# First layer's scatters limited to four under way, and two expert set-ups with other buffers and loads

## The reference

```python
xn = layernorm(x)
x = x + L0_attn(xn) + L0_ffn(xn)      # gated linear attention (8 heads, chunks of 64) with its own
                                      # gated hidden layer; 14 experts of 176 hidden, best 2 of each token,
                                      # and a shared expert of 352 hidden
xn = layernorm(x)
x = x + L1_attn(xn) + L1_ffn(xn)      # state space model, 48 heads of 64, state 128;
                                      # 16 experts of 96 hidden, best 2 of each token
```

## Time and profile before

| | us |
|---|---|
| three runs | 3090.74, 3104.93, 3109.07 |
| median | 3104.93 |
| the profiled execution, its own time | 3097.32 |
| its span, first to last instruction | 3095.5 |
| mean granted TensorE clock | 0.938 of full |

### The profile page before, as it was taken

One profiled execution on the slowest core, in us unless ns is written; L12 is line 12 of the kernel. 1 busy time (PEld: TensorE's weight loads), 2 busy tenths in 40 slices (PEclk: granted clock), 3 DMA queues, 4 the chain that ended last, 5 costly groups with the idle time before them and its releaser, 6 DMA issues.

```text
span 3095.5 us, 58605 instructions
## 1 busy us (share of the span) xinstructions
PE 2693.5 (87%) x17318; PEld 2112.8 (68%) x17318; DVE 2383.3 (77%) x5972; ACT 2125.2 (69%) x4682; POOL 1976.0 (64%) x1697
## 2 busy tenths in 40 slices
PE   3698889886739978378799999999999999999997
PEld 2366666664539855267578788787787878878786
DVE  2466666664457769657699999999899999999996
ACT  3454454541245556445489999999899999999996
POOL 2232212225304413555489999999999999999998
PEclk8799898997869999689899999999999999999999
DMA  5455455464566545445777786666766666666663
GB/s 135 110 180 171 152 185 172 149 203 151 179 178 200 170 169 157 163 135 175 222 255 234 225 254 207 214 206 208 228 205 214 207 213 220 204 216 204 200 216 115
DMA packets 320411, 588.35 MB, mean 190 GB/s; under 512 B 47863, under 2 KB 138775, under 8 KB 319607
## 3 DMA queue, kind: packets, MB, share of 16 engines
q1 hardware_dynamic: 305750, 545.07, 56.5%
q0 software_dynamic: 14352, 39.54, 3.4%
HBM read 464.44 MB, written 124.17 MB: 190 GB/s over the span
## 4 chain that ended last, share of the span: by engine, by line
POOL 35%; issue 10%; ACT 3%; DVE 2%; POOLq 1%; PE 1%; DMA 0%; SPq 0%; ACTq 0%; DVEq 0%
POOL mm L2684 8%; POOL y L2697 7%; POOL yz L2701 7%; POOL y_lo L2690 6%; POOL y L2711 6%; ACT mt L2614 1%; DVE cv L2767 1%; POOLq L2360 1%; ACT ys L2628 0%; ACT mt L2634 0%; DVE bank L2838 0%; ACT L2649 0%; POOL first L2726 0%; DMA wi<-ssm_wi_split 0%; DVE xd L2829 0%
## 5 line engine op out<-in xcount | busy, mean ns | idle before, releaser
L2684 POOL TENSOR_TENSOR mm<-mt,cb 128x512 f32<-128x512 f32 x384 | 492.5, 1305 | 56.0 <-ACT mt L2634 53.8
L2614 ACT ACTIVATE mt<-a_wide,a_tok 128x128 f32<-128x128 f32 x1536 | 487.1, 389 | 3.2 <-POOL mm L2684 2.5
L2767 DVE SCALAR_TENSOR_TENSOR cv<-bank,taps,cv 128x509 f32<-128x509 f32 (+2 forms) x576 | 429.7, 746 | 13.6
L64 PE MATMUL bank<-f,wi 128*128 128x512 f32 x768 | 321.6, 419 | 15.9 <-DMA wi<-ssm_wi_split 15.9
L66 PE MATMUL bank<-f,wi 128*128 128x512 f32 x768 | 304.9, 397 | 0.0
L65 PE MATMUL bank<-f,wi 128*128 128x512 f32 x768 | 304.9, 397 | 0.0
L2701 POOL TENSOR_TENSOR yz<-y,zs 128x512 f32<-128x512 f32 x192 | 249.0, 1297 | 15.1
L2690 POOL TENSOR_TENSOR y_lo<-yz,y_hi 128x512 fp32r<-128x512 f32 x192 | 246.6, 1285 | 8.5 <-ACT y_hi L2639 6.6
L2697 POOL TENSOR_TENSOR y<-t 128x512 f32<-128x512 f32 x192 | 246.4, 1283 | 0.0
L2507 PE MATMUL bank<-mm,x_tok 128*64 128x128 f32 x3072 | 226.9, 283 | 13.3 <-POOL mm L2684 13.3
L2711 POOL TENSOR_TENSOR y<-y,ys 128x512 f32<-128x512 f32 x184 | 237.2, 1289 | 0.0
(11 more groups left out here) (476 smaller groups left out, 8063.2 us busy)
## 6 DMA issues: line engine op xcount, KB each, us to landing
wi<-ssm_wi_split SPq DMA_DIRECT2D x192, 512.0 KB
a_wide<-a_scratch SPq DMA_DIRECT2D x192, 512.0 KB
l_fw<-ffn_split SPq DMA_DIRECT2D x72, 768.0 KB
ea<-ea_scratch SPq DMA_DIRECT2D x384, 128.0 KB
wo<-ssm_wo_split SPq DMA_DIRECT2D x192, 256.0 KB
sorted_scratch<-ex_zeros SPq DMA_DIRECT2D x96, 130.5 KB
ssm_wi_split<-l_s_out SPq DMA_DIRECT2D x24, 512.0 KB
ey_x<-sorted_scratch SPq DMA_DIRECT2D x94, 130.5 KB
```

The source lines that it names most:

```text
L64: pe.matmul(out, wh, xh, start=first, stop=False)
L2614: i = act.activation(mt[:, h, chunk(j)], a_wide[:, g % R, h, chunk(j)], ACT.Relu, bias=a_tok[:, s * NJ + j, 2 * t + h:2 * t + h + 1], scal ...
L2684: pl.tensor_tensor(mm[:, :, ts], mt[:, :, ts], cb[:, js, :].rearrange("p j t -> p (j t)") .unsqueeze(1).broadcast_to([P, 2, TS // 2]), ALU ...
L2767: dve.scalar_tensor_tensor(cv[:, a:TS], bank[:, X, 0:TS - a], taps[:, t, k:k + 1], cv[:, a:TS], ALU.mult, ALU.add).then_inc(ph["tap"], 1)
```

## The change

1. In `layer0`, the 64 scatters count on the four `put` semaphores in turn (m % 4, with m the number of the scatter), and scatter m waits until scatter m - 4 has landed. `rows_back(i)` for i >= 4 waits for all four semaphores to show all scatters up to those of group i - 4. The last wait's number is the same total per semaphore.
2. In the set-up of `experts`, the ring holds 18 raw tiles instead of 12; the down weights are loaded after tiles 5 and 11, each half in two transfers, of 80 and of 8 partitions, and are split after tiles 5 and 11 (before: 4 and 8).
3. In the set-up of `experts1`, the eight tiles without a place of their own lie in the first 16 sets of `x_all`, whose rows have been sent, instead of in the down weights' place; SP waits once for the first batch's scatters and no longer for the down weights' low part.

```diff
--- before.py
+++ after.py
@@ -480,7 +480,8 @@
                     else:
                         done(sp, "placed", 0, PLACE_OPS)
                     if i >= RX:
-                        sp.wait_ge(swdge[f"put{i % RX}"], i // RX * 2 * RX * 16)
+                        for q in range(4):
+                            sp.wait_ge(swdge[f"put{q}"], (i - RX + 1) * RX // 2 * 16)
                     sp.dma_start(group[i % RX][:, :, 0:D], rows_dram[i * RX * P:(i + 1) * RX * P].rearrange("(r p) d -> p r d", p=P))\
                         .then_inc(swdge[f"group{i % RX}"], 16)
 
@@ -943,8 +944,11 @@
                         pl.tensor_copy(group[i % RX][:, :, D:XW], ext[:, n:n + RX, :]).then_inc(ph["extra"], 1)
                         pl.wait_ge(ph["extra"], i + 1)
                     for c in range(2):
+                        m = 2 * n + c
+                        if m >= 4:
+                            pl.wait_ge(swdge[f"put{m % 4}"], m // 4 * 16)
                         pl.indirect_dma_start(sorted_dram[:], bass.IndirectOffsetOnAxis(ap=disp["place"][:, c, n:n + 1], axis=0),
-                                              group[i % RX][:, n % RX], None).then_inc(swdge[f"put{i % RX}"], 16)
+                                              group[i % RX][:, n % RX], None).then_inc(swdge[f"put{m % 4}"], 16)
 
                 def low(n):
                     if n is None:
@@ -986,7 +990,7 @@
                         for i in range(n):
                             scatter((k - G) * n + i)
                 for r in range(RX):
-                    pl.wait_ge(swdge[f"put{r}"], NG // RX * 32)
+                    pl.wait_ge(swdge[f"put{r}"], NG // 2 * 16)
 
             @block.vector
             def _(dve):
@@ -1282,7 +1286,7 @@
 
         gu_hi, gu_lo = sb("gu_hi", [P, E0, KD, GU], F32R), sb("gu_lo", [P, E0, KD, GU], F32R)
         wd_hi, wd_lo = sb("wd_hi", [HH, E0, 2, D], F32R), sb("wd_lo", [HH, E0, 2, D], F32R)
-        RG = 12
+        RG, WIDE, DOWN_AT = 18, 80, (5, 11)
         with ExitStack() as setup:
             raw = sb("raw", [P, RG, 2 * KD * P], F32, setup)
             wd_raw = sb("wd_raw", [HH, 2, E0, D], F32, setup)
@@ -1304,11 +1308,12 @@
                         if i >= RG:
                             sp.wait_ge(ph["low"], 2 * (i - RG + 1))
                         sp.dma_start(raw[:, i % RG, :], moe0[i, :, 0:2 * KD * P]).then_inc(ph[f"raw{i % RG}"], 16)
-                        if i == 3:
+                        if i == DOWN_AT[0]:
                             sp.wait_ge(swdge["ordered0"], NI * 16)
-                        if i in (3, 6):
-                            h = i // 6
-                            sp.dma_start(wd_raw[:, h], down_dram[h]).then_inc(ph[f"down{h}"], 16)
+                        if i in DOWN_AT:
+                            h = DOWN_AT.index(i)
+                            sp.dma_start(wd_raw[0:WIDE, h], down_dram[h, 0:WIDE]).then_inc(ph[f"down{h}"], 16)
+                            sp.dma_start(wd_raw[WIDE:HH, h], down_dram[h, WIDE:HH]).then_inc(ph[f"down{h}"], 16)
 
                 @block.scalar
                 def _(act):
@@ -1316,9 +1321,9 @@
                         act.wait_ge(ph[f"raw{i % RG}"], (i // RG + 1) * 16)
                         for k in range(KD):
                             act.activation(columns(gu_hi, i, k), tile_of(i, k), ACT.Copy).then_inc(ph["high"], 1)
-                        if i in (4, 8):
-                            h = i // 8
-                            act.wait_ge(ph[f"down{h}"], 16)
+                        if i in DOWN_AT:
+                            h = DOWN_AT.index(i)
+                            act.wait_ge(ph[f"down{h}"], 32)
                             act.activation(wd_hi[:, :, h, :], wd_raw[:, h], ACT.Copy).then_inc(ph["down_high"], 1)
 
                 @block.vector
@@ -1990,7 +1995,7 @@
             raw = sb("raw", [P, RG, 2 * KD * P], F32, setup)
             wd_all = sb("wd_all", [P, NE, D], F32, setup)
             wd_raw = wd_all[0:HH]
-            more = wd_all[:].rearrange("p e d -> p (e d)").rearrange("p (i w) -> p i w", i=NI - RG)
+            more = x_all[:, 0:NG, :].rearrange("p n d -> p (n d)")[:, 0:(NI - RG) * 2 * KD * P].rearrange("p (i w) -> p i w", i=NI - RG)
             ph = Phase(nc, pool)
 
             def columns(w, i, k):
@@ -2016,9 +2021,9 @@
                         sp.dma_start(wd_raw[:, half(h)], down_dram[:, half(h)]).then_inc(ph[f"down{h}"], 16)
                         for i in range(h * RG // 2, (h + 1) * RG // 2):
                             sp.dma_start(place(i), moe1[i, :, 0:2 * KD * P]).then_inc(ph[f"raw{i}"], 16)
+                    for q in range(4):
+                        sp.wait_ge(swdge[f"sent0{q}"], NG // 2 * 16)
                     for i in range(RG, NI):
-                        if (i - RG) % 4 == 0:
-                            sp.wait_ge(ph["down_low"], (i - RG) // 4 + 1)
                         sp.dma_start(place(i), moe1[i, :, 0:2 * KD * P]).then_inc(ph[f"raw{i}"], 16)
 
                 @block.gpsimd
```

## The result

The changed kernel takes 3079.42 us (median of 4 runs, 3073.31 to 3084.25), the kernel before beside it 3104.59 (4 runs). The ratio is 0.9917, 95% interval 0.9896 to 0.9937: 25 us faster. The profiled execution of the changed kernel took 3077.26 us around a span of 3075.5; that of before had a span of 3095.5, so the pair of profiles shows 20.0 us.

A forecast was written before the change was run, and what follows sets the result against it. The prediction took late PE signals during unchecked scatters to cost some 40 us in the first layer, with GpSimd's last stage untouched. Gains of 23 + 7 + 1 = 31 us from 3100.5 gave 3069, range 3044 to 3095.

The forecast's parts named there:

- Part 1, gain 23: First layer's 64 scatters: limit of four removes late PE signals; 1.6 us each, block ends at 828, not 851.4.
- The signs that were named: First layer: no remote wait above 6 us, PE share near 0.85 at full clock, scatters 1.5 to 1.7 us apart.
- Part 2, gain 7: First set-up: larger ring and down weights cut at partition 80 end it at 891.5 in place of 898.8.
- the 3 us that the text gave: First set-up: gain of 3 if loads still crowd the tiles and the second down load lands 4 us later.
- VectorE is then the bound: First set-up: after the 7 us gain, VectorE's work was to set the end, at 891.5.
- the 26 us that the text had named: First set-up: a second down load landing no earlier than 26 us after the start would show the forecast wrong.
- the estimate after the Trainium skill's rule: First set-up: busiest DMA engine carries 6 rows a load, not 8; part 2 gains 9 us in place of 7.
- Part 3, gain 1: Second set-up: eight tiles issued earlier, GpSimd still ends the block; 1 us gained, between a loss of 2 and gain of 3.
- the same bytes only come in another order: Second set-up: with DMA engines 0.93 busy, earlier tiles only reorder traffic, so the gain is 1 us.
- The limit does nothing: Rival on the first layer's scatters: limit of four never holds, late signals stay; gain 4 to 12, about 3092; chance 0.18.
- A pace of 1.9 us: Rival on the first layer: scatters at 1.9 us end the block at 847; gain 12, 3088; chance 0.11.
- the turning point of 1.96 us: First layer, slower rival: beyond this time per scatter the block ends later than before; 3120 at 2.4 us; chance 0.06.

The follow-up runs named there:

- eight under way: Part 1 alone, but with eight scatters under way in place of four, against the kernel before: 3104.0 us, ratio 1.0002 (chip 6).
- the second profile: The changed kernel run again, unaltered, on chip 6, against the kernel before: 3078.9 us, ratio 0.9910.
- the first pair: Profiles of the changed kernel and the kernel before from their first timing: spans of 3075.5 and 3095.5 us; ratio of the runs 0.9917.
- part 1 alone: The kernel before with only the limit of four scatters under way added: 3055.5 us, ratio 1.0011 (chip 9).
- two under way: The limit of part 1 alone, set to two scatters in place of four: 3103.6 us in one run, kernel before 3106.0 (chip 2).
- one pause: The kernel before with one GpSimd memset and a wait for it ahead of each scatter, no limit: 3096.8 us, ratio 0.9976 (chip 2).
- the first comparison: The changed kernel's first timing against the kernel before, chip not known: 3079.4 against 3104.6 us, ratio 0.9917.
- two pauses: Kernel before plus two waited memsets per scatter: 3053.7 us, ratio 1.0003 (chip 13); also with part 2, down weights first: 3067.7 us, 0.9887 (chip 2).

## Why the prediction was right, and where it was not

**The base and the sum.** 3069 was forecast, within 3044 to 3095; 3079.4 was measured. Of the 31 us of the sum, 24.2 + 3.0 - 3.1 = 24.1 are found in the stages. The forecast is 10 us low: 4 us of the base, a mean of 3100.5 over four executions where the comparison's median was 3104.6, and 6 of the sum, 31 against the 25 us between the medians. That the number lies so near is in part luck: part 1 carries nearly all of it, the two others missed, and on chips 9 and 13 the same kernel should, by its stages, gain nothing.

**Part 1, gain 23; measured 24.2.** The reading of the stall was right: signals of PE that come late while scatters follow each other unchecked. The pace, too: 1.6 us taken, 1.66 measured, and the scatters end the block, not PE. Two things in it were only half the truth. It spoke of a limit; eight under way is a limit and does nothing, while two memsets without any written limit do the same as four under way. And it took the stall for a property of the kernel. On chips 9 and 13 there is none, and part 1 costs some 2 to 3 us of the stretch instead. The signs that were named hold: no remote wait, 1.5 to 1.7 us a scatter, the last scatter opens the set-up. PE's share was 48.45 / 58 = 0.84 at a clock of 0.91, not quite the full clock.

**Part 2, gain 7; measured 3.0, and 4.4 in the second profile.** This step failed. It left the gain at the low end, the 3 us that the text gave for a second load 4 us later. "VectorE is then the bound" doesn't hold: ScalarE and VectorE wait for the down loads, and the second landed 26.7 us after the start, which is past the 26 us that the text had named as the sign of being wrong; VectorE ended 39.9 us after it, not within 36. A down load was costed at 6 us by 211 GB/s; from 841.08 to 853.20 it took 12, behind the tiles ahead of it. And the sum had 4 us from the second landing to VectorE's last tiles; it took 7.0 (865.03 to 872.06), ScalarE's 3.19 and VectorE's 3.89 one after the other. The ring did what it should (SP waits for nobody up to tile 17), but the wait was handed to the loads. The cut is worth about 2 us. That is what the estimate after the Trainium skill's rule added for it (page "DMA: Bandwidth & Descriptors", section "Why a DMA increments its semaphore by 16 and not by 1"): 9 us in place of 7 for the whole of part 2. The trace agrees in size; what is missing is the 7, which was to come from ring and order. Two windows of 2 us in this stretch still pass 122 and 159 GB/s at shares of 0.99 and 0.97:

```profile
850.00:852.00 2.00, 0.00 (x0) 0.00 (x0) 0.00 (x0) 0.00 (x0) 0.00 (x0) 0.50 0.99 122
862.00:864.00 2.00, 0.00 (x0) 0.00 (x0) 1.93 (x7) 0.00 (x0) 0.00 (x0) 0.50 0.97 159
```

The sum also left out that the DMA engines are full for most of the set-up: from 840 to 868 every window of 2 us has a share of 0.89 or more, whatever the order of the loads.

**Part 3, gain 1; measured a loss of 3.1 in the first pair, 2 us between neighbours on chip 9, 0 to 1 us against the old set-up on chips 2 and 6.** The step that failed is "the same bytes only come in another order". They come earlier, VectorE does eight tiles in one unbroken run, and that run keeps GpSimd from its next scatter. How much of this the old set-up already had differs: its longest record is 3.71 or 3.72 us in the kernel before and on chips 9 and 13, 4.39 on chips 2 and 6. That the block ends with GpSimd was in the text; what would delay GpSimd wasn't.

**Rivals.** "The limit does nothing" is what chip 9 shows, for a reason that the rival didn't have: no late signals there to take away. Its own reason fails: the limit does hold (2.22 us of waiting at 739.08), and a landing, put at 2.3 us there, takes 2.4 us at the least and 5.4 us on the median of the 64 scatters of part 1 alone. A pace of 1.9 us and more came only with two under way (2.11 us, stretch 136.3), which lies on the far side of the turning point of 1.96 us: that kernel lost 3 us of the stretch against before, where 64 steps of 2.11 would make 10.

**What stays open.** Which property of a chip makes PE's signals late, and whether the number under way acts beside the step: the beats of the second layer are slow on chip 6 at three scatters in 5 us, but in bursts of three. What makes a down load slow was not separated either: its rows, its partitions or its source.

One thing sets the late chips apart in the traces themselves. The 64 scatters tell of their landing by 1024 updates of semaphores. The traces of chips 9 and 13 hold 1021 to 1024 of them, those with the stall (before, eight under way, one pause) 273 to 347, the other five of the late chips 542 to 888. Over all semaphores, what is missing lies between the first and the last indirect DMA of the program: there the late chips' traces hold 10,371 to 11,323 updates and the others 15,726 to 15,878, while before it (5450 to 5453) and behind it (24,609 to 24,614) all fourteen agree. What delays the signals may be what loses their records, and whether the recording of the trace has a part in the stall was not tested: that rival stands.

The changed kernel itself was never timed on chip 9 or 13; from its stages there (2 to 3 us lost in the stretch, 3 won in set-up 1, 2 lost in set-up 2) it should be even or 1 to 2 us slower, as an estimate.

## What to carry to other kernels

A stall in which several engines wait for signals that one engine must long have sent, beside idle DMA engines, is not cured by more room or by fewer waits; look for what issues closest beside it, and space that or limit it: here a smallest step between scatters of 1.51 us in place of 1.35 took the stretch from 128.8 us to 104.8 on the same chip. Time both versions on more than one chip before calling such a stall a property of the kernel: the same kernel took 3052 and 3104 us. And before work is moved earlier, ask what runs unbroken because of it, and whom that run keeps out.

## What was not expected of the hardware

- Two groups of chips under the same kernel: medians of the kernel before of 3050.9 and 3052.2 us (chips 13 and 9), and 3098.8 to 3106.0 (chips 2 and 6 and the first comparison). Two stretches of scatters account for it, some 28 us in the first layer and some 21 us in the second experts. On the second group the traces also hold fewer updates of semaphores for the same work, 40,435 to 41,390 against 45,785 to 45,941, with all of the difference in the stretch where scatters run.
- On the second group an engine waited up to 17.29 us on a signal of PE while scatters started every 1.3 to 1.5 us, and never so with four or two under way or with two pauses.
- A scatter issued beside VectorE's subtractions with both inputs in SBUF lasts until 0.84 us after the last of them, and one that starts beside the single long subtraction of 2.29 us until 0.84 us after that one; beside the same with one input in a PSUM bank, 0.96 to 1.03 us.
- A memset and a wait for it cost GpSimd 0.1 us per scatter (smallest step 1.35 us for 1.26), not the 0.4 that was expected: the wait fits into the 0.30 us that it stands idle between two scatters.
